# Gathers of y at the destinations taken out of the node pass and into the edge pipeline, with six accumulation rounds in place of ten in the edge stage

## What is computed

```python
# third layer: messages along the edges, summed per target row
h = x @ W_in2f
Wij = (shifted_softplus(f_ij @ W_f1 + b_f1) @ W_f2 + b_f2) * rcut_ij[:, None]
y = segment_sum(h[idx_j] * Wij, idx_i, num_segments=N_ATOMS)   # idx_i = src, idx_j = dst
out = shifted_softplus(y @ W_o1 + b_o1) @ W_o2 + b_o2
# fourth layer: two rounds of neighbour means
agg = segment_sum(x[src], dst, num_segments=n)
h = relu(mean @ Wl.T + bl + x @ Wr.T)
```

## Time and profile before

| what | us |
|---|---|
| time, median of 3 runs | 2957.11 |
| lowest and highest | 2956.41 and 2964.25 |
| the profiled execution: time | 2955.35 |
| the profiled execution: span of the trace | 2953.6 |

### The profile page before, as it was taken

How to read it: one execution, slowest core, us unless ns; L and a number is a source line. 1 busy time by engine, 2 the same in 40 slices (tenths; PEclk the granted TensorE clock), 3 DMA queues, 4 the chain that set the end, 5 groups by cost and what they waited for, 6 DMA issues and landing times. The chain is left out here.

```text
span 2953.6 us, 46939 instructions
## 1 busy us (share of the span) xinstructions
PE 2277.4 (77%) x14558; PEld 1881.0 (64%) x14558; DVE 1971.0 (67%) x2850; ACT 1788.2 (61%) x3704; POOL 1615.1 (55%) x1214
## 2 busy tenths in 40 slices
PE   4888878887888879997889399788896888833443
PEld 3777777777777757775666277677774666623333
DVE  5667666666666756665788389788895898833332
ACT  4666666666666647776566177677775888821111
POOL 5865443455444034442688665788860334348887
PEclk9999999999999889998899699899998999965555
DMA  3544334343333268886788567688884666634332
GB/s 104 114 116 115 96 103 128 100 130 97 97 102 106 79 179 254 253 252 180 177 207 203 120 145 165 158 226 229 221 211 118 195 201 203 199 99 110 99 99 68
DMA packets 335885, 447.30 MB, mean 151 GB/s; under 512 B 121203, under 2 KB 174153, under 8 KB 335000
## 3 DMA queue, kind: packets, MB, share of 16 engines
q1 hardware_dynamic: 215336, 380.38, 44.5%
q0 software_dynamic: 120000, 63.45, 11.8%
q10 hardware_dynamic: 304, 0.49, 0.0%
HBM read 252.28 MB, written 192.56 MB: 151 GB/s over the span
## 5 line engine op out<-in xcount | busy, mean ns | idle before, releaser
L584 DVE TENSOR_REDUCE g_ss<-g_sq 125x4 f32<-125x1024 f32 x125 | 151.8, 1215 | 240.8 <-ACT g_sq L511 240.7
L377 POOL DMA_INDIRECT g_xd<-in_x,idx x100 | 122.8, 1228 | 318.3 <-PE banks L484 293.6
L1635 POOL DMA_INDIRECT out<-em_c,to_s x100 | 135.8, 1358 | 293.9 <-DVE em_c L1951 268.0
L1584 POOL DMA_INDIRECT combined<-acc,idx x200 | 257.9, 1290 | 64.0 <-issue 60.7
L447 PE MATMUL banks<-mats,g_hT 128*125 128x256 f32 x1000 | 281.4, 407 | 0.0
L1565 POOL DMA_INDIRECT acc<-combined,first_ x100 | 209.2, 2092 | 113.5 <-DMA acc<-combined,first_ 62.9
L444 PE MATMUL banks<-bias_y,ones 128*125 128x512 bf16 x250 | 105.4, 422 | 178.6 <-DVE g_z L590 132.3
L467 PE MATMUL banks<-mats,g_zT 128*125 128x128 f32 x2000 | 238.7, 273 | 0.0
L467 PEld LDWEIGHTS banks<-mats,g_zT 128*125 128x125 f32 x2000 | 228.3, 188 | 0.0
L447 PEld LDWEIGHTS banks<-mats,g_hT 128*125 128x125 f32 x1000 | 203.1, 203 | 32.2 <-issue 0.6
L590 DVE TENSOR_TENSOR g_z<-banks,g_rs 125x512 f32<-125x512 f32 x250 | 161.1, 686 | 87.6 <-ACT g_rs L522 87.6
(11 more groups left out here) (355 smaller groups left out, 7172.3 us busy)
## 6 DMA issues: line engine op xcount, KB each, us to landing
x<-g_x SPq DMA_DIRECT2D x125, 224.0 KB
g_x<-in_xT SPq DMA_DIRECT2D x100, 250.0 KB
acc<-g_zero SPq DMA_DIRECT2D x101, 224.0 KB
gin_x<-x SPq DMA_DIRECT2D x50, 448.0 KB
h<-gin_hr SPq DMA_DIRECT2D x50, 448.0 KB
al_h<-h SPq DMA_DIRECT2D x50, 448.0 KB
al_x<-x SPq DMA_DIRECT2D x50, 448.0 KB
out<-al_out SPq DMA_DIRECT2D x50, 448.0 KB
```

What stands on the lines that cost most here:

```text
L584: nc.vector.reduce_sum(SS[q % 2][:, :], SQ[q % 2][:, :, :], AX.X).then_inc(red, 1)
L1584: pool.indirect_dma_start(out=CR[:, m % 6, r * D:r * D + D], out_offset=None, in_=K.acc, in_offset=bass.IndirectOffsetOnAxis(ap=idx[:, g, ...
```

## The change

The 25 gathers of y at the destinations leave the node stage. They are now issued by POOL in the second edge stage, from `acc` straight into the tile em_yd, which has four buffers in place of three. The table `y_of_dst`, its 25 stores in the node stage and its 25 loads in the second edge stage are gone. ROUNDS is 6 in place of 10, so that 19 rounds in place of 15 are left for the node stage. The gathers of h in the edge stage keep their rule (two behind each round, the rest at the end), and what was `nodes_alone` is a class, `Nodes`, whose stages are called in the same order. The place of the `keep`s that are left is the same formula.

```diff
-        for m in range(2 * EG):
-            idx, _, g = of(m)
+        for m in range(EG):
             past_slot(pool, kept, m - 6, 32)
             for r in range(R):
                 pool.indirect_dma_start(out=CR[:, m % 6, r * D:r * D + D], out_offset=None, in_=K.acc,
-                                        in_offset=bass.IndirectOffsetOnAxis(ap=idx[:, g, r:r + 1], axis=0)).then_inc(got[m % 6], 16)
+                                        in_offset=bass.IndirectOffsetOnAxis(ap=K.src[:, m, r:r + 1], axis=0)).then_inc(got[m % 6], 16)
...
-                for i in range(NP + 4):
-                    if i < NP:
-                        load(i)
+                for i in range(count + 4):
+                    n.load(sp, i)
                     if i >= 4:
-                        store(i - 4)
-                    for m in range(2 * EG):
+                        n.store(sp, i - 4)
+                    for m in range(tables * EG):
                         if 20 + (3 * m) // 5 == i:
                             keep(sp, m)
...
-        X, H, Y, XD, YD = [sb(n, [P, R, D], k=3) for n in ("x", "h", "y", "xd", "yd")]
+        X, H, Y, XD = [sb(n, [P, R, D], k=3) for n in ("x", "h", "y", "xd")]
+        YD = sb("yd", [P, R, D], k=4)
...
-                for k in range(EG):
+                def get(k):
+                    past(pool, ydT, k - 4)
+                    for r in range(R):
+                        pool.indirect_dma_start(out=YD[k % 4][:, r, :], out_offset=None, in_=K.acc,
+                                                in_offset=bass.IndirectOffsetOnAxis(ap=K.dst[:, k, r:r + 1], axis=0)).then_inc(got[k % 4], 16)
+
+                def put(k):
                     past(pool, done, k)
                     past_slot(pool, sent, k - 1, 16 * R)
...
+                steps(EG, [(0, get), (5, put)])
...
                 def load_d(k):
-                    past(sp, ydT, k - 3)
                     past(sp, bd, k - 3)
                     past(sp, me, k - 3)
-                    move(sp, flat(YD[k % 3]), slots_of(K.yd, k), din[k % 3])
...
                 def turn_yd(k):
-                    past_slot(pe, din, k, 80)
+                    past_slot(pe, got, k, 16 * R)
...
-        ROUNDS = 10
+        ROUNDS, PAIRS = 6, NG // 2
...
-        nodes_alone(nc, K, out, side, keep, kept_all)
+        nodes_alone(nc, K, out, PAIRS, side, keep, kept_all, 1)
```

More of the change, by code:

```diff
@@ L1106, in halves, with __init__ @@
     return tile[:, :, :].rearrange("p (h r) d -> p h (r d)", h=2)
[L1109 to L1114, removed]
+class Nodes:
+    def __init__(self, nc, K, out, name, ctx, first, count, banks):
         def sb(n, shape, dt=F32, k=2):
@@ L1127, in nodes_alone @@
[L1127 to L1132, removed]
+        self.nc, self.K, self.table, self.begin, self.count = nc, K, out, first, count
+        self.pH, self.pA, self.pX, self.pU, self.pC = banks
+        self.X, self.H, self.OUT = [sb(n, [P, 2 * R, D], k=3) for n in ("x", "h", "out")]
@@ new lines, in half, with load, store @@
+    def half(self, tile, h):
+        return tile[:, R * h:R * h + R, :]
+    def load(self, sp, k):
+        if k < self.count:
+            past(sp, self.a, 2 * (k - 3) + 1)
+            past(sp, self.hT, 2 * (k - 3) + 1)
+            move(sp, halves(self.H[k % 3]), pair_of(self.K.h, self.begin + k), self.xin[k % 3])
+            move(sp, halves(self.X[k % 3]), pair_of(self.K.x1, self.begin + k), self.xin[k % 3])
+    def store(self, sp, k):
+        if k < self.count:
+            past(sp, self.done, k)
+            move(sp, pair_of(self.table, self.begin + k), halves(self.OUT[k % 3]), self.stored[k % 3])
@@ new lines, in all_stored, with turn @@
+    def all_stored(self, sp):
+        for i in range(3):
+            sp.wait_ge(self.stored[i], 32 * ((self.count - i + 2) // 3))
+    def turn(self, pe, k, h):
+        if k < self.count:
+            t = 2 * k + h
+            past_slot(pe, self.xin, k, 64)
+            past(pe, self.bt, t - 1)
+            for j in range(R):
+                m = self.nc.tensor.transpose(self.pH[:, P * j:P * j + P], self.H[k % 3][:, R * h + j, :], self.K.ident[0:P, 0:P])
+            m.then_inc(self.hT, 1)
@@ L1134, in nodes_alone, with on @@
+def on(stage, eng, *h):
+    return lambda k: stage(eng, k, *h)
+def nodes_alone(nc, K, out, count, side, keep, kept_all, tables):
+    ctx = ExitStack()
+    with ctx:
+        n = Nodes(nc, K, out, "al", ctx, 0, count, (K.ps[0], K.ps[1:3], K.ps[3:5], K.ps[5], K.pairs[3]))
         with nc.Block() as block:
@@ L1179, in turn_x3 @@
[L1179 to L1203, removed]
```

241 lines of the change are left out of this document (146 added, 95 removed).

## The result

The changed kernel takes 2982.02 us in the median of 3 runs (2979.17 to 2986.11), where the kernel before took 2957.11: the ratio is 1.0078, with a 95% interval of 1.0048 to 1.0109. It is slower, by 24.9 us, where +13.4 was forecast; the time lies inside the range of 2960 to 2984, 2 us from its upper end. In a later set of runs, with more runs of the kernel before beside it, the same kernel came to 1.0056 (1.0037 to 1.0075), or +14.2 us between the medians (2977.90 against 2963.66). The profiled execution took 2986.11 us, the slowest of its three, with a span of 2983.4.

A forecast was written before the change was run, and what follows sets the result against it. Stages were read singly: POOL ended the edge stage, SP's wait for gathers of y held up the nodes, compute bound the second edge stage. -32.0 + 49.2 - 5.8 + 2.0 = +13.4 us gave 2970.5 us, range 2960 to 2984.

The forecast's parts named there:

- Part 1: Edge stage: without four rounds compute ends it, so the node stage starts earlier; -32.0 us, between -34 and -30.
- that may add some 3 us and no more: End of edge stage: POOL's last gathers of h wait in a four-buffer ring for SP's stores, some 3 us at most.
- The barrier behind compute: End of edge stage: no transfer has to land behind ACT, so 0 to 3.66 us; 1.7 taken.
- Part 2: Node stage: four more rounds delay the first gathers of y, SP and pair 21's load; +49.2 us, between +47.6 and +56.
- The price of a round beside drained nodes: Node stage, rounds 16 to 19 beside no other transfer: 12.3 us each, with 11.9 and 14.0 as ends.
- Part 3: Node stage, steps 35 to 49: without gathers and stores of y_of_dst, pairs run at 10.30 us; -5.8 us, between -8 and -2.
- -2, the wait lay elsewhere: Smallest gain allowed for removing gathers and stores of y_of_dst from steps 35 to 49 of the node stage: -2 us.
- Part 4: Second edge stage: POOL's wait for DVE covers the gathers; only a later start is left, +2 us, between 0 and +5.
- rival B: Node stage: moved rounds cost 14 to 17 us each from the accumulation itself; total +20 to +32 us; chance 0.12.
- A: SP's queue at step 20: rounds get out of the way in time; -35.8 us, total 2921 us; chance 0.05.
- C: Whole kernel: gains and costs cancel to +6 us, within 0.3% (8.9 us) of no change, 2963 us; chance 0.24.
- D: Second edge stage: POOL's slowed instructions bound it, +19 us on top, +32 in all, 2989 us; chance 0.05.

The follow-up runs named there:

- the first pair: First profiled runs, chip number not known: kernel before at 2957.11 us, changed kernel at 2982.02 us, ratio 1.0078.
- the third set: Later runs on chip 6: kernel before 2963.66 us, profiled again 1.0014; changed 1.0056; stores from step 28 0.9834, with five buffers for gathers of h too 0.9838.
- the four kernels with five buffers: Changed kernel with five buffers, not four, for gathers of h: 1.0076; also stores from step 28: 0.9858 and 0.9838; four rounds, stores from 31: 0.9860.
- the first set: Follow-ups on chip 12, kernel before 2964.90 us: changed with stores from 28 0.9811 or ten rounds 0.9997; before with stores from 23 0.9912 or six rounds 1.0064.
- the second set: Follow-ups on chip 12, kernel before 2998.41 us: three changed kernels with five buffers for gathers of h, 1.0076, 0.9858, 0.9860; changed with stores from 24, 0.9954.

## Why the prediction was right, point by point

**What bounds the kernel.** Right in each stage. The step that carried the forecast was to follow POOL's queue through SP to the nodes, and not to take POOL's 40 us of rest at the end of the node stage as room. Moving the stores in the kernel before, with nothing else, gave 24 us of the total.

**Part 1, four rounds out of the edge stage.** -32.0 forecast; -27.9 in the first pair, -32.9 in the third set, -29.4 with the rounds alone. Inside its bounds of -34 to -30 in one of three. By the prediction's own sign (the node stage starting behind 1641) this part is wrong in the first pair, with 1643.36, and not in the third set, with 1639.7. The step that was mis-sized is "that may add some 3 us and no more, since SP's steps end with compute. So compute ends the stage": POOL did, by 3 to 6 us, because three groups were still to be gathered when the ring let it go at 1618.90, and a store's landing of 3.7 us stands behind the last. The barrier behind compute was priced at 1.7; in the four kernels with five buffers it is 1.1 in three and 1.5 in one.

**Part 2, four rounds into the node stage.** +49.2 forecast for the load of pair 21, +50.6 in the first pair, +46.4 in the third set (276.2 against 229.7), the latter 1.2 below the stated bounds. The price of a round beside drained nodes was 12.3 forecast and is 12.2. The fifteen rounds ahead of it took 213.2 us, 3.7 more than before, and the two gathers behind landed 1.7 us quicker; with 0.6 us less from the start of the first round and the price of the last four, 1.4 us are left. That these errors nearly cancel is luck.

**Part 3, no gathers behind step 34.** -5.8 forecast. From pair 30 to 47 the stores came at 10.30 for 10.67 us, -6.3. But behind the load of pair 21 the stage was only 1.0 us shorter, because pairs 22 to 30, paced by the gathers in both kernels, took 11.27 us each in place of 10.79: +3.9. In the third set the same stretch went the other way, 10.60 for 11.04, and the part came to -7.0. The step "-2, the wait lay elsewhere" was the bound that the first pair broke. What sets the pace in that stretch from run to run was not tried.

**Part 4, the gathers in the second edge stage.** +2 forecast, +4.6, +2.6, and +2.4 with ten rounds. The period held and the cover was as computed. The first em_yd was late by 1.0 us, as worked out, and the first scatter by 2.0 (54.2 us behind the stage's start, where it was 52.2). What was missing is at the end: from the start of the last scatter to the next stage it is 7.2 us in every kernel with the gathers and 5.9 in every one without (ten and four profiles). That 1.3 us is shown; what causes it is not. The last 1.2 lie between the first scatter and the last and are not there in the third set (0.1).

**The sum.** +13.4 forecast. By stages that the change touches, the first pair gives -27.9 + 49.6 + 4.6 = +26.3, the third set -32.9 + 39.4 + 2.6 = +9.1; the medians +24.9 and +14.2. The forecast lies between the pairs and nearer to the second: the mechanism was right, and the rest is terms that differ by 2 to 10 us from one pair to the next. In the first pair the loss was nearly twice the forecast. It lies above the +9 to +20 that had the chance of 0.54 and among the numbers given to rival B (+20 to +32), whose mechanism did not come about; parts 1, 3 and 4 each fell short by 2.6 to 4.8 us, all the same way. That the range held it is owed to its reach beyond the forecast as much as to the sum.

**The rivals.** A (the wait does not bind) is refuted by the 62 us. B (rounds stay dear) is refuted for this place by the 12.2 us, and its other half is true in the mean: in company a round costs 14.0 to 14.8 (means of nine profiles). C (terms cancel) did not come about, though the change's gathers alone are such a case; its sum of +6 should read +7.2 (-34 + 49.2 - 8 + 0), which changes nothing else. D (POOL bounds the second edge stage) did not come about: POOL still waited for DVE. The durations of POOL's instructions in that stage (ns, min/median/max), the first answering to the earlier trace rows:

```profile
L1709 POOL DMA_INDIRECT out<-em_c,to_s x100: 1187/1195/1930, 2321.6 to 2653.9; - x100
...
L1702 POOL DMA_INDIRECT em_yd<-acc,idx x100: 1205/1218/1706, 2268.2 to 2583.0; - x100
```

The longest scatter was 1.93 us and the longest gather 1.706. The Trainium skill ("SBUF — State Buffer", the box on the "DVE blocks DMA" trap and the section "A bandwidth-pool intuition that's wrong" behind it) has a DMA of GpSimd stretched from some 620 to 3100 ns beside a `tensor_copy` of DVE; no such stretch is in these rows. But they do not test the page: in this stage DVE runs no copy from one tile in SBUF to another (its single COPY, of em_hrd, and its TENSOR_SCALARs read `banks`, the matmul results), so the disagreement in size that the prediction saw is none. No run here shows which of DVE's operations would bring the stretch.

## The version that beats both

The changed kernel with its stores of y from step 28 takes 2909.50 and 2914.60 us in two sets, 0.9811 and 0.9834 of the kernel before. Stores from a later step alone gave 0.9912. Once the join is gone, the rounds moved out of the edge stage are the gain that the change was made to bring, some 28 to 35 us, and only the gathers in the second edge stage are paid for it, 2.6 to 6.2 us there. Whether the gathers had to be moved was not tried: no kernel has six rounds, all 50 gathers in the node stage and the stores from a later step. The trace of the kernel before with six rounds speaks for the move: there POOL starts its last gather of y 576.3 us behind the stage's start, having issued all 200 with 0.30 us between two, and the node stage of this version is over at 553.0 to 558.2.

## What to carry to other kernels

A queue that serves two pipelines is a join between them, even where neither looks busy: before moving work to an engine that rests at the end of a stage, find the first thing that anyone issues behind its result, and count from the stage's start to there, not to the stage's end. Here that wait already showed in the trace as 11.55 us, and each microsecond added ahead of it came out in full. And when work moves behind a hand-written place in a queue, the place has to move with it: here one constant made the difference between 1.006 and 0.983.

## What the runs showed of the hardware

- An accumulating indirect transfer of 4 x 125 rows, with the wait until it has landed, took 12.2 to 12.6 us with SP standing still (means of the last four rounds in four profiles, single ones from 11.9 to 13.6), and 14.0 to 14.8 beside the nodes' loads and stores (means of nine profiles, single ones from 11.7 to 22.8).
- The kernel before took 2964.90 us in the first set and 2998.41 in the second, 1.1% more, under one chip number; the third set, under another, had 2963.66. The granted clock over a whole run of it was 0.892 in the median in the first and third sets and 0.886 in the second. In the second set the second edge stage, with the gathers in it, took 406 to 412 us and the stretch ahead of the edge stage 1404.3 to 1408.0. What differed between the sets is not known.
- After 61 us without work PE took up work at 1929.13 at a granted clock of 0.50 (its level of 1.2 GHz). The window of 10 us in which it did so has 0.50, the next 0.81 and the one behind it 1.00, much as after the pause of 11.55 us before, with 0.50, 0.85 and 1.00. So the longer pause cost no more clock than the short one:

```profile
1922.00:1932.00 10.00, 1.92 (x8) 1.57 (x9) 0.00 (x0) 1.74 (x4) 7.93 (x7) 0.50 0.81 206
1932.00:1942.00 10.00, 10.00 (x64) 8.43 (x63) 5.99 (x6) 5.24 (x10) 8.11 (x7) 0.81 0.90 241
1942.00:1952.00 10.00, 8.99 (x70) 7.75 (x69) 9.38 (x9) 7.65 (x16) 8.15 (x7) 1.00 0.83 206
```

These are windows of the changed kernel: the stretch and its length, busy time of PE, PE's weight loads, DVE, ACT and POOL, then the granted clock, the share of the transfer engines and GB/s.
